# Turning the first two blocks of rows before the second permutation, in a one-core transformer kernel

## The chip, the cores and the metric

The kernel runs on one core of a Trainium2 chip. The metric is device microseconds for one execution, and the median of several executions is compared.

## The reference

The input x is 2 sequences of 1024 rows by 256 columns. Four steps follow one another; each adds its result, times the tanh of a gate, to x. What matters here is the second step, a mixture of experts with 2 of 16 experts for each row:

```python
x = x + tanh(g_xattn[0]) * attention(layernorm(x), ctx, ctx)
# second step, on h = layernorm(x), 2048 rows
scores = softmax(h @ gate_w); topk_w, topk_idx = top_k(scores, 2)
y = sum over the 2 picked e of topk_w * ((silu(h @ w1[e]) * (h @ w3[e])) @ w2[e])
x = x + tanh(g_ffn[0]) * (y + h)
x = x + tanh(g_xattn[1]) * linear_of(layernorm(x), mean of ctx)
x = x + tanh(g_ffn[1]) * ternary_mlp(layernorm(x))     # 256 -> 1024 -> 1024 -> 1024 -> 256
```

## The kernel before, in words

**Stages.** The attention and the routing take the first 66 us of the profile, the expert blocks come next, and four groups of 512 rows go through the last network. That last network is one long run of matmuls on TensorE.

**Blocks.** The 4096 picks (2048 rows, two experts each) are sorted by expert into up to 47 blocks of 128 rows (`NBLK`). The first 16 blocks are the first 128 picks of each expert, so that block i belongs to expert i; the other 31 (`NREST`) hold what is left. The list of a block's rows (`perm`) is made by a product of 0/1 matrices on TensorE, which the code calls a permutation: `ohr` says at which place in its block a pick stands, `ohf` and `ohb` say in which block. The first permutation (with `ohf`) fills the lists of the 16 blocks, the second (with `ohb`) those of the other 31. GpSimd reads the lists and fetches the rows of each block from HBM with an indirect DMA into one of six buffers (`xg`, `xg_more`).

**One block.** TensorE turns the 128 x 256 rows (`turns`, two transposes), ScalarE copies the high part out (`high_turned`), VectorE takes the remaining low part (`low`), and TensorE multiplies both with the expert's weights (`gate_up`, six matmuls). ScalarE's SiLU and VectorE's `product` follow, and the product rides along with the turning of a later block to the expert's second product (`down`). Loops on all engines run over i, the block, and `turns` is called two blocks ahead: `turns(0)` and `turns(1)` stand ahead of the loop.

**The order.** Every engine's work is written out by hand in one list. An engine takes its list in order, and semaphores make it wait for other engines. What the change touches stands at one place in the program, between the first permutation and the loop over the blocks:

- VectorE makes `ohb` in some 25 steps, then ten small steps compute the expert of each of the 31 blocks (`ecol`), then come `low(0)` and `low(1)`.
- TensorE fills waits with products that nobody reads, `keep_clock(bank, n)`: n calls of 128 x 128 by 128, each of which stands as two rows in the profile. It does the first permutation in two pieces with such fillers between them, fillers again, the second permutation, one small product for the experts' offsets (`pe_eoff`), two fillers, and the two turns.
- The turned halves lie in `turned0` to `turned5`, and `turned0` to `turned4` lie over `ohr`. The second permutation reads `ohr`, so with these buffers a turn can be copied out only after it.
- A turn waits for the rows that GpSimd fetched, and all turns stand behind a wait for `pool_step` 3, which GpSimd gives after it has issued the first fetch.

Of the kernel before, what the change touches and what calls it, by code (L numbers as in the profile page):

```python
# [29 lines left out]
P = 128  # L30
# [81 lines left out]
def flamingo_kernel(nc, x, ctxT, cols, rows, wq, wkT, wvT, gate, experts, w1T, w2T, panels, consts, identity, out):  # L112
    with ExitStack() as ctx:
# [89 lines left out]
        route_end = w_off + 4 * 4 * DK * D  # L203
        VT = put("VT", [P, DK, P])
# [9 lines left out]
        xT = put("xT", [P, 2, DK, GN])  # L214
# [64 lines left out]
        t_high, t_low = turned[0:3], turned[3:6]  # L279
        outb = nc.alloc_sbuf_tensor_at("outb", [P, TG, D], F32, offset=bl_off)  # L280
# [61 lines left out]
        bank_y, bank_first = [bank[6], bank[5]], bank[7]  # L342

# [404 lines left out]
        def _(eng):  # L748
# [276 lines left out]
            own(eng.tensor_scalar(bexp[:, :], pinc_0[:, :], 1.0 / P, kc[:, K_TOK:K_TOK + 1], ALU.mult, ALU.is_le))  # L1025
            own(eng.tensor_tensor(ends_0[:, :], count_0[:, 0:E], prest_0[0:1, :], ALU.add))
            own.done()
            own(eng.reduce_sum(ecol_0[:, :], bexp[:, :], AX.X))

            own(eng.scalar_tensor_tensor(count_0[:, 0:E], count_0[:, 0:E], float(P), ends_0[:, :], ALU.is_gt, ALU.mult))  # L1030
            own.done()
            own(eng.tensor_scalar(bexp[:, :], pinc[:, :], 1.0 / P, kc[:, K_TOK:K_TOK + 1], ALU.mult, ALU.is_le))
            own(eng.scalar_tensor_tensor(ecol_0[:, :], ecol_0[:, :], float(E), ecol_0[:, :], ALU.is_lt, ALU.mult))
            own.done()
            own(eng.reduce_sum(ecol[:, :], bexp[:, :], AX.X))
            own.done()
            own(eng.tensor_tensor(ecol[:, :], ecol[:, :], ecol_0[:, :], ALU.add))
            own.done()
            eng.tensor_scalar(ecol[:, :], ecol[:, :], float(E - 1), float(EXP_COLS), ALU.min, ALU.mult).then_inc(dve_ecol, 1)
            own(eng.reduce_max(end_0[:, :], count_0[:, :], AX.X))  # L1040

# [61 lines left out]
            def low(n):  # L1103
                b, w = n % 3, joint(n)
                eng.wait_ge(b_xh, n + 1)
                eng.tensor_tensor(t_low[b][:, w], bank_t[b][:, w], t_high[b][:, w].bitcast(F32),  # L1106
                                  ALU.subtract).then_inc(b_xl, 1)
# [60 lines left out]
            low(0)  # L1168
            low(1)
# [180 lines left out]
        def _(eng):  # L1350
# [126 lines left out]
            def high_turned(n):  # L1477
                b, w = n % 3, joint(n)
                eng.wait_ge(b_tx, n + 1)
                eng.activation(t_high[b][:, w], bank_t[b][:, w], ACT.Copy).then_inc(b_xh, 1)  # L1480
# [102 lines left out]
        def _(eng):  # L1583
# [205 lines left out]
            def first_there(r, t):  # L1789
# [49 lines left out]
            def gate_up(i, at_):  # L1839
                b = i % 3  # L1840
# [4 lines left out]
                for k in range(DK):  # L1845
                    w = bass.ds(at_ + k * 2 * H, 2 * H)
                    x_k = slice(k * P, (k + 1) * P)
                    ins = three(bank_gu[i % 2][:, 0:2 * H], (t_high[b][:, x_k], t_low[b][:, x_k]), (EH[:, w], EL[:, w]),
# [42 lines left out]

            eng.wait_ge(act_setup, ACT_LATE + 2)

            eng.wait_ge(pool_step, 3)
            keep_clock(bank[5], 2)
            turns(0)
            turns(1)
            for i in range(NBLK + DOWN):
                expert_there(i)
                if i < 2:  # L1900
                    gate_up(i, offsets[i])
                    turns(i + 2)
                else:
# [240 lines left out]
```

## Time and profile before

| what | us |
|---|---|
| median of 3 executions | 500.75 |
| the three executions | 500.48, 500.75, 505.57 |
| the profiled execution's own time | 505.3 |
| its span, first to last instruction | 503.2 |
| time of the profiled execution outside the span | 2.1 |

The granted clock of TensorE has two levels in the profile, 1.00 (2.4 GHz) and 0.50 (1.2 GHz); its mean over the span is 0.975. A stretch at the lower level makes TensorE's work there take about twice as long. The profiled execution is one of the longer ones: it lies 4.55 us above the median, and near the longest of the three.

### The profile page before, as it was taken

Reading aid. Unit: us, or ns where it says so; the run is one execution under the profiler, and the core shown is the slowest. Engines: PE = TensorE matmul, PEld = TensorE weight load, DVE = VectorE, ACT = ScalarE, POOL = GpSimd, SP = SyncE. Lnnn points to the kernel's source line nnn. Section 1 sums busy time; section 2 is a strip of 40 time slices with the busy share of each in tenths; the row PEclk is TensorE's granted clock in tenths of the full one; section 3 lists DMA queues with packets and bytes.
Section 4 is the critical chain, followed back from the end, with each engine's and each line's share of the span. In section 5 each row is a group of like instructions: output and inputs, shape, how many; then the busy total and the mean of one; then the engine's idle time right before and its main releaser. Section 6 shows DMA issues by size and latency. Waiting matters only on the chain.

```text
span 503.2 us, 7823 instructions
## 1 busy us (share of the span) xinstructions
PE 482.0 (96%) x2742; PEld 415.2 (83%) x2742; DVE 317.0 (63%) x848; ACT 217.9 (43%) x444; POOL 150.7 (30%) x157
## 2 busy tenths in 40 slices
PE   8898979998798999999999999999999999999996
PEld 8787769997787788888978888887888898788885
DVE  4868886875686766656476776346875634654523
ACT  4568935775467876411362221236112223511210
POOL 1667867747870411100260111044110101000000
PEclk9879977999999999999999999999999999999999
DMA  8944833797663578212050320022132002022101
GB/s 294 350 173 139 283 122 105 221 305 230 203 190 115 178 261 271 64 42 85 3 167 21 106 63 2 0 70 98 24 102 64 1 1 83 4 81 66 40 1 49
DMA packets 34465, 58.82 MB, mean 117 GB/s; under 512 B 4529, under 2 KB 18353, under 8 KB 34354
## 3 DMA queue, kind: packets, MB, share of 16 engines
q1 hardware_dynamic: 29760, 47.12, 28.9%
q0 software_dynamic: 3840, 10.49, 7.3%
q10 hardware_dynamic: 818, 0.61, 0.5%
q8 instruction: 25, 0.41, 0.4%
q14 instruction: 22, 0.18, 0.1%
HBM read 47.85 MB, written 14.42 MB: 124 GB/s over the span
## 4 chain that ended last, share of the span: by engine, by line
PE 84%; DVE 8%; POOL 3%; DMA 2%; issue 2%; ACT 0%; SPq 0%; DVEq 0%
PE bank L2015 23%; PE bank L2016 23%; PE bank L1984 6%; PE bank L1987 6%; PE bank L1588 3%; PE bank L1590 3%; PE bank L1589 3%; PE bank L2048 3%; PE bank L2047 3%; PE bank L1833 2%; DMA xg<-xb_dram,perm 2%; PE bank L1648 1%; PE bank L1681 1%; DMA gw<-gate 1%; POOL y_first L623 1%
## 5 line engine op out<-in xcount | busy, mean ns | idle before, releaser
L1562 ACT ACTIVATE sg<-bank,colv 128x512 f32<-128x512 f32 x64 | 44.1, 690 | 176.6 <-PE bank L2016 176.6
L2015 PE MATMUL bank<-Ah,Wr 128*128 128x512 f32 x256 | 100.2, 391 | 0.0
L2015 PE MATMUL bank<-Bh,Wr 128*128 128x512 f32 x256 | 99.9, 390 | 0.0
L2016 PE MATMUL bank<-Al,Wr 128*128 128x512 f32 x256 | 99.7, 390 | 0.0
L2016 PE MATMUL bank<-Bl,Wr 128*128 128x512 f32 x256 | 99.7, 389 | 0.0
L2015 PEld LDWEIGHTS bank<-Ah,Wr 128*128 128x128 f32 x256 | 48.0, 188 | 11.1 <-DVE Al L1275 0.8
L2016 PEld LDWEIGHTS bank<-Bl,Wr 128*128 128x128 f32 x256 | 48.1, 188 | 9.9
L2015 PEld LDWEIGHTS bank<-Bh,Wr 128*128 128x128 f32 x256 | 48.1, 188 | 9.8
L2016 PEld LDWEIGHTS bank<-Al,Wr 128*128 128x128 f32 x256 | 48.1, 188 | 9.7
L1288 DVE CAST Ah<-sg 128x512 fp32r<-128x512 f32 x32 | 13.6, 425 | 60.1 <-ACT sg L1562 60.1
L1588 PE MATMUL bank<-EL,turned 128*128 (+1 forms) x141 | 44.9, 319 | 0.9 <-DVE turned L1106 0.6
L565 POOL TENSOR_TENSOR rstd<-veps,mhalf 128x4 f32<-128x4 f32 x6 | 8.4, 1399 | 107.9 <-DVE veps L745 61.1
L1590 PE MATMUL bank<-EH,turned 128*128 (+1 forms) x141 | 40.5, 287 | 0.0
L1589 PE MATMUL bank<-EH,turned 128*128 (+1 forms) x141 | 40.5, 287 | 0.0
L1548 ACT ACTIVATE sg<-bank,colv 128x512 f32<-128x512 f32 x32 | 22.1, 690 | 38.1 <-PE bank L1987 37.6
L1271 DVE SCALAR_TENSOR_TENSOR sg<-bank,colv,sg 128x512 f32<-128x512 f32 x32 | 24.0, 751 | 22.9 <-ACT sg L1548 22.6
L1288 DVE CAST Bh<-sg 128x512 fp32r<-128x512 f32 x32 | 13.6, 426 | 38.6 <-ACT sg L1562 38.6
L1984 PE MATMUL bank<-xTh,Wr 128*128 128x512 f32 x96 | 37.7, 393 | 0.0
L1987 PE MATMUL bank<-xTl,Wr 128*128 128x512 f32 x96 | 37.6, 392 | 0.0
L642 POOL DMA_INDIRECT xg<-xb_dram,perm x32 | 31.3, 979 | 10.1 <-issue 6.0
L1480 ACT ACTIVATE turned<-bank 128x384 fp32r<-128x384 f32 (+2 forms) x51 | 23.8, 467 | 20.4 <-PE bank L1836 11.6
L1106 DVE TENSOR_TENSOR turned<-bank,turned 128x384 fp32r<-128x384 f32 (+2 forms) x51 | 26.6, 521 | 9.3 <-ACT turned L1480 9.0
(286 smaller groups left out, 1039.8 us busy)
## 6 DMA issues: line engine op xcount, KB each, us to landing
Wraw<-panels SPq DMA_DIRECT2D x44, 256.0 KB, 4.0
stage<-panels SPq DMA_DIRECT2D x44, 256.0 KB, 2.7
ES<-experts SPq DMA_DIRECT2D x16, 384.0 KB, 5.4
ys_dram<-yb SPq DMA_DIRECT2D x47, 128.0 KB, 2.7
ys_dram<-x SPq DMA_DIRECT2D x1, 1920.0 KB, 8.7
X<-x SPq DMA_DIRECT2D x3, 512.0 KB, 7.1
xb_dram<-xb SPq DMA_DIRECT2D x3, 512.0 KB, 5.3
out<-outb SPq DMA_DIRECT2D x3, 512.0 KB, 3.3
```

The costliest lines, as they stand in the source:

```text
L642: eng.indirect_dma_start(out=rows, out_offset=None, in_=xb_dram, in_offset=bass.IndirectOffsetOnAxis(ap=perm[:, i:i + 1], axis=0)).then_in ...
L1106: eng.tensor_tensor(t_low[b][:, w], bank_t[b][:, w], t_high[b][:, w].bitcast(F32), ALU.subtract).then_inc(b_xl, 1)
L1271: eng.scalar_tensor_tensor(sg[:, m % 3, :], bank[2 * (m % 2) + 1][:, :], colv[:, C_S2 + m:C_S2 + m + 1], sg[:, m % 3, :], ALU.mult, ALU.mu ...
L1288: own(eng.tensor_copy(h[0][:, m, :], sg[:, r, :]))
L1562: eng.activation(sg[:, (8 * layer + m) % 3, :], bank[m % 4][:, :], ACT.Gelu, scale=colv[:, c + m:c + m + 1]).then_inc(f_act[m], 1)
L1588: mm(dst, lhs[0], rhs[1], start=first, stop=False)
L1589: mm(dst, lhs[1], rhs[0], start=False, stop=False)
L1590: return mm(dst, lhs[0], rhs[0], start=False, stop=last)
L1984: mm(dst, w[:, u, k, :], x_high[:, k, :], start=k == 0, stop=False)
L1987: ins = mm(dst, w[:, u, k, :], x_low[:, k, :], start=False, stop=k == DK - 1 and not general)
L2015: mm(bank[m % 4][:, :], Wr[:, base:base + P], h[0][:, k, :], start=k == 0, stop=False)
L2016: ins = mm(bank[m % 4][:, :], Wr[:, base:base + P], h[1][:, k, :], start=False, stop=k == FK - 1 and not general)
```

## The change

Two pairs of buffers, `first_high` and `first_low`, take the turned halves of blocks 0 and 1. They lie where `xT` of the attention lay, which is moved to the front of its region for that, so `ohr` is no longer in the way. On TensorE `turns(0)` and `turns(1)` stand ahead of the second permutation. The fillers are 8 in place of 4 between the pieces of the first permutation, and 9 and 10 in place of 12 ahead of the second; the 2 after it are gone. The small product for the offsets goes behind `turns(3)`. On VectorE the ten `ecol` steps stand behind `low(0)`, ahead of `low(1)`.

```diff
+        put = over(route_end, e_off)
+        first_high, first_low = ([put(f"{n}{b}", [P, DK * P], F32R) for b in range(2)] for n in ("first_high", "first_low"))
...
+        def turned_pair(n):
+
+            return (first_high[n], first_low[n]) if n < 2 else (t_high[n % 3], t_low[n % 3])
...
@@ VectorE
-            own(eng.tensor_scalar(bexp[:, :], pinc_0[:, :], 1.0 / P, kc[:, K_TOK:K_TOK + 1], ALU.mult, ALU.is_le))
...
-            own(eng.reduce_max(end_0[:, :], count_0[:, :], AX.X))
...
             low(0)
+            own(eng.tensor_scalar(bexp[:, :], pinc_0[:, :], 1.0 / P, kc[:, K_TOK:K_TOK + 1], ALU.mult, ALU.is_le))
...
+            own(eng.reduce_max(end_0[:, :], count_0[:, :], AX.X))
             low(1)
...
@@ TensorE
                     if t == NT - TG:
-                        keep_clock(bank[5], 4)
+                        keep_clock(bank[5], 8)
                         eng.wait_ge(dve_ohf, NG)
...
-            keep_clock(bank[5], 12)
...
-            permutation(bank_y[0][:, 0:NREST], lambda r, t: ohb[:, r, :, t], rest_there)
-
-            eng.wait_ge(dve_ecol, 1)
-            mm(bank_first[0:1, 0:NREST], ecol[:, :], ident[:, 0:NREST], start=True, stop=True).then_inc(pe_eoff, 1)
...
+            keep_clock(bank[5], 9)
             eng.wait_ge(act_setup, ACT_LATE + 2)
-
             eng.wait_ge(pool_step, 3)
-            keep_clock(bank[5], 2)
+            keep_clock(bank[1], 10)
             turns(0)
             turns(1)
+            permutation(bank_y[0][:, 0:NREST], lambda r, t: ohb[:, r, :, t], rest_there)
             for i in range(NBLK + DOWN):
...
                     turns(i + 2)
+                    if i == 1:
+                        eng.wait_ge(dve_ecol, 1)
+                        mm(bank_first[0:1, 0:NREST], ecol[:, :], ident[:, 0:NREST], start=True, stop=True).then_inc(pe_eoff, 1)
```

This is TensorE's list before, from the first permutation (`ohf`) to the first block's gate/up products. `xg_more` and `xg` with `ident` are the turns, `ohb` is the second permutation, and a call of `keep_clock` is one `bank<-ident`:

```order
L1786 MATMUL bank<-ohf,ohr 128x16 x24
L1595 MATMUL bank<-ident 128x128 x4
L1786 MATMUL bank<-ohf,ohr 128x16 x8
L1595 MATMUL bank<-ident 128x128 x12
L1786 MATMUL bank<-ohb,ohr 128x31 x32
L1814 MATMUL bank<-ident,ecol 1x31
L1595 MATMUL bank<-ident 128x128 x2
L1833 MATMUL bank<-ident,xg_more 128x128 x2
L1833 MATMUL bank<-ident,xg 128x128 x2
L1588 MATMUL bank<-EL,turned_183 128x256
```

And the same place after the change, where the lines of the code stand about six further on:

```order
L1792 MATMUL bank<-ohf,ohr 128x16 x24
L1601 MATMUL bank<-ident 128x128 x8
L1792 MATMUL bank<-ohf,ohr 128x16 x8
L1601 MATMUL bank<-ident 128x128 x19
L1831 MATMUL bank<-ident,xg_more 128x128 x2
L1831 MATMUL bank<-ident,xg 128x128 x2
L1792 MATMUL bank<-ohb,ohr 128x31 x32
L1594 MATMUL bank<-EL,first_high_189 128x256
```

The two turns moved ahead of the permutation, with all the fillers ahead of them, and the gate/up product of block 0 stands right behind the permutation.

This is VectorE's list after the change, from the end of `ohb` to the first `product`; before it, rows `bexp` to `end_173` stood directly behind `ohb`:

```order
L1027 TENSOR_TENSOR ohb<-kbrep,pblk_143 128x496 x2
L1096 TENSOR_TENSOR first_low_191<-bank,first_high_189 128x256
L1158 TENSOR_SCALAR bexp<-pinc_163,kc 128x16
...
L1172 TENSOR_SCALAR ecol<-ecol 128x1
L1173 TENSOR_REDUCE end_173<-count_172 1x1
L1096 TENSOR_TENSOR first_low_192<-bank,first_high_190 128x256
L1100 TENSOR_TENSOR bh<-bank,bsg 128x128
```

The low part of block 0 now stands ahead of the expert steps, that of block 1 behind them.

## Rows read from the trace of the kernel before

**Rows 1.** The page, part 4: engines' shares of the chain that ended last.

```profile
PE 84%; DVE 8%; POOL 3%; DMA 2%; issue 2%; ACT 0%; SPq 0%; DVEq 0%
```

**Rows 2.** Windows: length, then PE, PEld, DVE, ACT, POOL busy; PEclk, DMA, GB/s.

```profile
21.20:31.40 10.20, 10.20 (x43) 9.43 (x42) 7.12 (x34) 5.06 (x14) 8.12 (x11) 0.50 0.85 306
31.40:65.50 34.10, 30.94 (x259) 25.67 (x259) 28.37 (x122) 30.93 (x71) 25.67 (x34) 1.00 0.57 185
65.50:72.40 6.90, 5.80 (x32) 5.41 (x32) 6.30 (x32) 1.70 (x3) 2.86 (x4) 0.51 0.28 88
72.40:75.80 3.40, 2.66 (x38) 2.52 (x39) 2.41 (x13) 0.00 (x0) 2.53 (x3) 1.00 0.40 119
75.80:82.60 6.80, 6.20 (x30) 5.83 (x29) 2.87 (x10) 2.58 (x7) 4.71 (x5) 0.50 0.32 97
82.60:110.00 27.40, 27.40 (x236) 27.34 (x236) 23.38 (x70) 20.70 (x57) 19.52 (x19) 1.00 0.74 228
```

**Rows 3.** The chain that ended last, 73 to 84 us: start, us, what.

```profile
73.14 2.06 PE bank L1786 x32
75.19 0.15 PE bank L1814 x2
75.34 0.70 PE bank L1595 x4
76.04 0.44 PE bank L1833 x2
...
76.51 0.39 ACT turned L1480
...
76.92 0.43 DVE turned L1106
...
77.49 0.55 PE bank L1588
...
82.52 0.21 PE bank L1588
82.74 0.12 PE bank L1589
```

**Rows 4.** Timeline of TensorE: start, us, work, [idle before it, ended by].

```profile
41.45 0.20 PE L1689 MATMUL bank<-both,tri 128*128 128x64 f16 x1 [1.25 <-DVE both L842]
...
62.76 1.14 PE L1595 MATMUL bank<-ident 128*128 128x128 f32 x8
65.45 0.25 PE L1786 MATMUL bank<-ohf,ohr 128*128 128x16 f16 x4 [1.55 <-DVE ohr L894]
66.25 0.28 PE L1786 MATMUL bank<-ohf,ohr 128*128 128x16 f16 x4 [0.56 <-DVE ohr L894]
66.38 5.47 PE L1595 MATMUL bank<-ident 128*128 128x128 f32 x24
73.14 2.06 PE L1786 MATMUL bank<-ohb,ohr 128*128 128x31 f16 x32 [1.29 <-DVE ohb L1021]
...
83.86 0.38 PE L1833 MATMUL bank<-ident,xg_more 128*128 128x128 f32 x2
```

**Rows 5.** Timeline of VectorE at the same place.

```profile
72.58 0.74 DVE L1021 TENSOR_TENSOR ohb<-kbrep,pblk 128x496 f16<-128x496 f16 x2
73.24 0.23 DVE L1025 TENSOR_SCALAR bexp<-pinc,kc 128x16 f32<-128x16 f32 x1
...
74.89 0.15 DVE L1040 TENSOR_REDUCE end<-count 1x1 f32<-1x17 f32 x1
```

**Rows 6.** Timeline of GpSimd: issues of the fetches, and a later wait.

```profile
69.14 1.29 POOL L642 DMA_INDIRECT xg_more<-xb_dram,perm  x1 [3.43 <-DMA xb_dram<-xb]
70.73 1.06 POOL L642 DMA_INDIRECT xg<-xb_dram,perm  x1 [0.30 <-issue]
...
77.09 0.94 POOL L642 DMA_INDIRECT xg_more<-xb_dram,perm  x1 [0.30 <-PE bank L1833]
...
112.74 1.16 POOL L623 DMA_INDIRECT y_first<-ys_dram,slots  x1 [4.69 <-DMA ys_dram<-yb]
```

**Rows 7.** The tile xg between 60 and 84 us: its DMA from issue to landing.

```profile
DMA to landing us min/median/max: 2.8/2.8/2.8
```

More of the change, by code:

```diff
@@ L203, in flamingo_kernel @@
         route_end = w_off + 4 * 4 * DK * D
+        xT = put("xT", [P, 2, DK, GN])
         VT = put("VT", [P, DK, P])
@@ L213, in flamingo_kernel @@
         ones128 = put("ones128", [P, P])
-        xT = put("xT", [P, 2, DK, GN])
         xb = put("xb", [P, 2, TG, D])
@@ L1022, in _ @@
                                   pblk16[:, r, :].unsqueeze(1).to_broadcast([P, NREST, NT]), ALU.is_equal).then_inc(dve_ohb, 1)
-            own(eng.tensor_scalar(bexp[:, :], pinc_0[:, :], 1.0 / P, kc[:, K_TOK:K_TOK + 1], ALU.mult, ALU.is_le))
[L1026 to L1039, printed above, removed]
-            own(eng.reduce_max(end_0[:, :], count_0[:, :], AX.X))
             def block_experts():
@@ L1104, in low @@
                 b, w = n % 3, joint(n)
+                high_, low_ = turned_pair(n)
                 eng.wait_ge(b_xh, n + 1)
-                eng.tensor_tensor(t_low[b][:, w], bank_t[b][:, w], t_high[b][:, w].bitcast(F32),
-                                  ALU.subtract).then_inc(b_xl, 1)
+                eng.tensor_tensor(low_[:, w], bank_t[b][:, w], high_[:, w].bitcast(F32), ALU.subtract).then_inc(b_xl, 1)
             def product(i):
@@ L1168, in _ @@
             low(0)
+            own(eng.tensor_scalar(bexp[:, :], pinc_0[:, :], 1.0 / P, kc[:, K_TOK:K_TOK + 1], ALU.mult, ALU.is_le))
+            own(eng.tensor_tensor(ends_0[:, :], count_0[:, 0:E], prest_0[0:1, :], ALU.add))
+            own.done()
+            own(eng.reduce_sum(ecol_0[:, :], bexp[:, :], AX.X))
+            own(eng.scalar_tensor_tensor(count_0[:, 0:E], count_0[:, 0:E], float(P), ends_0[:, :], ALU.is_gt, ALU.mult))
+            own.done()
+            own(eng.tensor_scalar(bexp[:, :], pinc[:, :], 1.0 / P, kc[:, K_TOK:K_TOK + 1], ALU.mult, ALU.is_le))
+            own(eng.scalar_tensor_tensor(ecol_0[:, :], ecol_0[:, :], float(E), ecol_0[:, :], ALU.is_lt, ALU.mult))
+            own.done()
+            own(eng.reduce_sum(ecol[:, :], bexp[:, :], AX.X))
+            own.done()
+            own(eng.tensor_tensor(ecol[:, :], ecol[:, :], ecol_0[:, :], ALU.add))
+            own.done()
+            eng.tensor_scalar(ecol[:, :], ecol[:, :], float(E - 1), float(EXP_COLS), ALU.min, ALU.mult).then_inc(dve_ecol, 1)
+            own(eng.reduce_max(end_0[:, :], count_0[:, :], AX.X))
             low(1)
@@ L1479, in high_turned @@
                 eng.wait_ge(b_tx, n + 1)
-                eng.activation(t_high[b][:, w], bank_t[b][:, w], ACT.Copy).then_inc(b_xh, 1)
+                eng.activation(turned_pair(n)[0][:, w], bank_t[b][:, w], ACT.Copy).then_inc(b_xh, 1)
             def silu(i):
@@ L1839, in gate_up @@
             def gate_up(i, at_):
-                b = i % 3
+                high_, low_ = turned_pair(i)
                 eng.wait_ge(b_xl, i + 1)
@@ L1847, in gate_up @@
                     x_k = slice(k * P, (k + 1) * P)
-                    ins = three(bank_gu[i % 2][:, 0:2 * H], (t_high[b][:, x_k], t_low[b][:, x_k]), (EH[:, w], EL[:, w]),
+                    ins = three(bank_gu[i % 2][:, 0:2 * H], (high_[:, x_k], low_[:, x_k]), (EH[:, w], EL[:, w]),
                                 k == 0, k == DK - 1)
```

## The prediction

> **What bounds the kernel now.** I read the chain of waits first, from the end back. TensorE holds 84% of it [rows 1], so whatever lets TensorE reach its dense work sooner, or gives it a faster clock, should move the end, and work of other engines counts only where TensorE stands still for it. Next come the windows, for the granted clock. TensorE is at half clock in two places near the change, 65.5 to 72.4 us and 75.8 to 82.6 us, with full clock in the 3.4 us between [rows 2]. In the first nothing but fillers and waits is at stake. In the second it does the first blocks' real products, 6.20 us of work in 6.80 us, and each six-matmul product costs double: a matmul follows the last after 0.21 us at half clock and after 0.12 us at full [rows 3].
>
> Then the chain itself, piece by piece between 73 and 78 us [rows 3]. The second permutation runs from 73.14 to 75.19, the small product for the offsets takes 0.15, the two fillers 0.70, two of the four transposes 0.44, and then the chain leaves TensorE: ScalarE copies the high part of block 0 (76.51), VectorE takes the low part (76.92), and gate/up of block 0 starts at 77.49. So 2.30 us pass between the permutation's end and the first product (77.49 - 75.19), for work that needs nothing from the permutation. Ahead of it TensorE has stood 1.29 us for `ohb` [rows 4], after 5.47 us of fillers. The transposes would fit there if the rows of blocks 0 and 1 have come.
>
> **When the turns can run after the change.** Three things hold them up: the fillers ahead of them, the rows, and `pool_step`.
>
> The rows: GpSimd issues the fetch of block 0 at 69.14 and that of block 1 at 70.73 [rows 6]; a fetch lands 2.8 us after its issue [rows 7]. Block 0 is there at about 71.9 and block 1 at 73.53. Nothing ahead of these two fetches changes. GpSimd's signal comes behind the first issue, at 69.14 + 1.29 = 70.43.
>
> The fillers: 24 rows, 12 calls, took 5.47 us at half clock [rows 4], or 0.456 us for a call, and so about 0.228 at full. The nine calls from 66.38 end at 70.48 at half clock and at 68.43 at full; the ten calls behind the signal then start at about 70.45 in either case. At full clock they end at 72.7. At half clock until 72.4, as now, 4.2 calls fit before that and the other 5.8 take 1.3 us: 73.7. At half clock all the way they end at 75.0.
>
> With full clock the turns of block 0 end at 72.95 and TensorE waits for block 1 until 73.53; its turns end at 73.75 (0.22, half of the 0.44 of [rows 3]). `ohb` is ready at 73.00 for its first half and at 73.3 for its second [rows 3, 5], so the permutation starts at 73.75 and ends at 75.80 (its 2.05 us of now). That is 0.6 us later than now. With the clock as now up to 72.4, the turns end at 74.2 and the permutation at 76.25.
>
> Which of the two? Between 62.8 and 66.4 TensorE now stands 1.55 and 0.56 us, with four fillers' 1.14 us ahead [rows 4], and the clock falls by 65.5 to 65.6 [rows 2]. Four more calls fill 0.91 of the 1.55. The nearest row on the other side is the wait of 1.25 us at 41.45, through which the clock held [rows 4, 2]; 0.64 us idle is less than that, so I take the full clock. The doubt is worth 76.25 - 75.80 = 0.45 us, and a new idle time of about 2 us opens between the nine and the ten fillers (68.43 to 70.43), longer than the 1.25 that I know to be harmless.
>
> **Engines beside it.** ScalarE is idle from its table load on, so the high part of block 0 is done by 73.4. `low(0)` waits for it at the head of VectorE's list, behind `ohb` which ends at 73.3, and is done at 73.85 (its 0.43). What is queued behind it on VectorE is the ten steps of `ecol`, now 73.24 to 75.04 [rows 5], where VectorE then idles until 76.92. They now run from about 73.85 to 75.65, and `low(1)` ends at 76.1. Who waits for that? Gate/up of block 1, at 75.80 + 0.72 + 0.22 = 76.7 or later (six matmuls at 0.12, the turns of block 2), so the 1.8 us are still hidden; the cover goes if the first turns come after 74.5. The product for the offsets stands behind `turns(3)`, needs `ecol` of 75.6, and keeps its 0.15 us. The fetches of blocks 2 to 5 are issued as now. The other buffers' places and the copy of the low part into `first_low` cost nothing: same shapes, same engines.
>
> **First term, the order.** Gate/up of block 0 finds its low part ready since 73.85 and starts with the end of the permutation at 75.80 in place of 77.49: 1.69 us. Checked by pieces: 2.30 us between permutation and product go, less the 0.6 us by which the permutation starts later. With the slower fillers it is 77.49 - 76.25 = 1.24.
>
> **Second term, the clock in the blocks.** Now the clock falls at 75.8, at the end of a stretch with 2.66 us busy of 3.40 [rows 2], most of it the permutation's narrow matmuls (31 columns), and comes back at 82.6, some 5.1 us after the first product. The changed kernel has the same permutation there, and nearly the same wait, so I expect the fall again. But then TensorE has dense products at once, where it now begins with fillers, transposes and the wait for turned halves until 77.49. The shortest stretch at one level in the rows is 3.4 us [rows 2]; I estimate that the half clock lasts 3.4 us from 75.8 in place of 6.8. Products now spend 5.1 us at half clock, then 3.4, and half of the difference is gained: 0.86 us. The bounds are a half clock of the same 6.8 us, which loses (6.8 - 5.1)/2 = 0.85 of the first term, and no fall at all, which gains 5.1/2 = 2.55. I take the value in between because the wait inside the stretch is gone but the permutation before it is not.
>
> **Sum.** 1.69 + 0.86 = 2.55 us. In the trace that brings the turns of block 6 from 83.86 [rows 4] to 81.3. They need the fetch issued at 77.09 [rows 6], there at 79.9, so the supply holds and caps the whole gain at about 4. From 82.6 on TensorE has no idle time up to 110 [rows 2]; the following wait of GpSimd for the stored results (4.69 us at 112.74 [rows 6]) is for blocks that TensorE finishes, and so moves with it. I expect all of the 2.55 us at the end.
>
> **One rule weighed.** The second fetch sets the start of the permutation: 70.73 + 2.8 = 73.53 [rows 6, 7]. The Trainium skill, DMA: Bandwidth & Descriptors, section Anatomy of one DMA, gives a GpSimd DMA about 2.0 us plus its bytes at 436 GB/s, an estimate of 2.3 us for these 128 KB. By it the rows would be there at 73.0 and the first term would be 2.2 us; the trace has 2.8, and I keep that.
>
> **Against which time.** The profiled execution took 505.3 us, 4.55 above the median, so by its own time the changed kernel would show 502.75. The clock was at half for 10.20 us from 21.2 on [rows 2], before anything that the change touches, and half of that, 5.1 us, is about what lies between the two short executions (500.48, 500.75) and the longest. I take it that the short ones did not fall there. The change has no part in it, but it may set on which side a median falls. From the median: 500.75 - 2.55 = 498.2.
>
> **The rivals.** *The clock never falls.* If the fillers and turns keep the clock up through the permutation, the gain is 1.69 + 2.55 = 4.2, capped at 4 by the supply: 496.7. For it speaks that more of the stretch ahead is filled; against it, that the permutation's 2.05 us of narrow work and a wait remain.
>
> *The order helps, the clock takes it back.* The fall comes as now and lasts as long: 1.69 - 0.85, or 1.24 - 0.85 with slow fillers, 0.4 to 0.8: 500.1. Or the early turns gain nothing because block 1's rows land later than the eight other fetches say; then 500.5.
>
> *Slower: fillers ahead of the work.* The ten calls stand directly ahead of `turns(0)`. If the clock is low all the way from 65.5, they end at 75.0, the turns at 75.9, the permutation at 78.0 and gate/up starts at 78.1, 0.6 us late; if the clock then comes back one 3.4 us stretch later than now, at 86.0, products spend 7.9 us at half clock in place of 5.1, or 1.4 us more. Together 2.0 us: 502.8. It decides once the fillers end after 74.9. For it speaks the idle time of 2 us; against it, that 5.47 us of fillers brought the clock back at 72.4, and that the new list has more of them.
>
> *The median on the long side.* Two of four executions seen are at 505.3 to 505.6. With 2.55 gained the median would be 502.8 if most of the measured ones fall at 21 us.
>
> **How the numbers follow.** Forecast, gain 1.5 to 3.5: 0.45. No fall: 0.15. Little or nothing, 0 to 1.5: 0.15. Slower fillers: 0.08. Long side: 0.17. Predicted time 498.2. The range leaves out the lower end of the no-fall case and the worst of the last two: 496.0 to 503.2. A measurement of this kernel can tell about 1% (5 us) from no change, as the three times before spread by that much. Faster by over 1% needs 495.7: the no-fall case with luck in the executions, 0.09. Slower by over 1% needs 505.8: slow fillers and the long side together, 0.05. Within 1%: 0.86.
>
> **What the profile after would show.** The turns of blocks 0 and 1 end near 73.75, with a wait for the fetch of block 1 ahead of the second. The permutation follows without a wait for `ohb`, and gate/up of block 0 directly behind it with no wait for `first_low`. VectorE's `low(0)` is ahead of `bexp`, and nobody waits for `low(1)`. The half clock before the blocks is gone or shorter, and the one behind the permutation ends near 79. The turns of block 6 come near 81.3. I am wrong if ten fillers end after 74, if gate/up of block 1 waits for VectorE, or if a clock fall as long as 6.8 us follows gate/up of block 0.

## The result and the profile after

The changed kernel takes 497.78 us, the median of 22 executions (496.02 to 503.03); the kernel before takes 500.54 us beside it (22 executions, 499.08 to 505.72). The ratio is 0.9946, with a 95% interval of 0.9923 to 0.9968: a gain of 2.76 us, and between 1.6 and 3.9 by the interval. The forecast was 498.2.

The profiled execution took 501.49 us with a span of 499.6, 3.6 less than the span before. First the windows, with the columns of [rows 2]. The lines of the code stand some six further on than before.

```profile
8.00:14.80 6.80, 6.47 (x31) 6.48 (x32) 5.04 (x18) 2.54 (x6) 3.12 (x5) 0.50 1.05 378
...
65.50:72.40 6.90, 5.27 (x44) 4.69 (x44) 6.28 (x31) 1.70 (x3) 2.64 (x3) 1.00 0.22 65
72.40:75.80 3.40, 2.63 (x39) 2.62 (x39) 2.44 (x14) 0.77 (x2) 2.48 (x4) 1.00 0.33 101
75.80:82.60 6.80, 6.80 (x61) 6.57 (x60) 5.68 (x16) 4.62 (x13) 5.28 (x6) 1.00 0.39 115
82.60:110.00 27.40, 26.64 (x227) 26.25 (x226) 22.60 (x70) 20.72 (x56) 19.14 (x20) 1.00 0.85 261
```

Both half-clock stretches beside the change are gone: 61 matmuls between 75.8 and 82.6 us where [rows 2] have 30. There is one new thing in the last row: 0.76 us of idle time in 27.4, where TensorE had none. The timeline of TensorE after (start, us, work, idle before and what ended it) answers to [rows 4]:

```profile
65.76 0.26 PE L1792 MATMUL bank<-ohf,ohr 128*128 128x16 f16 x4 [0.56 <-DVE ohr L900]
65.87 2.25 PE L1601 MATMUL bank<-ident 128*128 128x128 f32 x18
69.08 2.47 PE L1601 MATMUL bank<-ident 128*128 128x128 f32 x20 [0.95 <-POOLq L652]
71.97 0.44 PE L1831 MATMUL bank<-ident,xg_more 128*128 128x128 f32 x2 [0.42 <-DMA xg_more<-xb_dram,perm]
73.17 0.44 PE L1831 MATMUL bank<-ident,xg 128*128 128x128 f32 x2 [0.77 <-DMA xg<-xb_dram,perm]
73.45 2.06 PE L1792 MATMUL bank<-ohb,ohr 128*128 128x31 f16 x32
75.32 0.37 PE L1594 MATMUL bank<-EL,first_high 128*128 128x256 f32 x1
...
79.66 0.38 PE L1831 MATMUL bank<-ident,xg_more 128*128 128x128 f32 x2
...
90.14 0.41 PE L1831 MATMUL bank<-ident,xg 128*128 128x128 f32 x2 [0.49 <-DMA xg<-xb_dram,perm]
...
97.61 0.41 PE L1831 MATMUL bank<-ident,xg_more 128*128 128x128 f32 x2 [0.27 <-DVE turned L1096]
...
115.03 0.41 PE L1831 MATMUL bank<-ident,xg_more 128*128 128x128 f32 x2 [1.81 <-DMA xg_more<-xb_dram,perm]
```

The order is as written: fillers, the two turns, the permutation, and the product of block 0 with no wait at all. The chain of waits (start, us, what) now reaches the permutation through the fetch of block 1, and no longer through VectorE and ScalarE as in [rows 3]:

```profile
63.90 4.48 DMA xb_dram<-xb
...
69.15 0.96 POOL xg_more L648
70.11 0.30 issue
70.41 2.72 DMA xg<-xb_dram,perm
73.17 0.44 PE bank L1831 x2
73.61 1.89 PE bank L1792 x32
75.51 0.18 PE bank L1594
```

VectorE's timeline, against [rows 5]: the low part of block 0 follows `ohb` at once, the last of the ten steps is over at 74.75, and the low part of block 1 comes behind it; no row of TensorE waits for either.

```profile
72.05 0.74 DVE L1027 TENSOR_TENSOR ohb<-kbrep,pblk 128x496 f16<-128x496 f16 x2
72.86 0.42 DVE L1096 TENSOR_TENSOR first_low<-bank,first_high 128x256 fp32r<-128x256 f32 x1
...
74.60 0.15 DVE L1173 TENSOR_REDUCE end<-count 1x1 f32<-1x17 f32 x1
74.68 0.40 DVE L1096 TENSOR_TENSOR first_low<-bank,first_high 128x256 fp32r<-128x256 f32 x1
```

GpSimd's fetches and its later wait, against [rows 6]:

```profile
69.15 0.96 POOL L648 DMA_INDIRECT xg_more<-xb_dram,perm  x1 [3.93 <-DMA xb_dram<-xb]
70.41 0.94 POOL L648 DMA_INDIRECT xg<-xb_dram,perm  x1 [0.30 <-issue]
...
108.97 0.99 POOL L629 DMA_INDIRECT y_first<-ys_dram,slots  x1 [2.74 <-DMA ys_dram<-yb]
```

**One mark to measure from.** Executions reach the change at different times, so absolute times of two traces can't be subtracted. All places below are therefore counted from the start of the last four matmuls of the first permutation (66.25 us before, 65.76 after), which both lists have and behind which the change acts. "First product" is gate/up of block 0, "turns 6" the turns of block 6, "y of 15" the end of ScalarE's copy of block 15's result, "fetch of y" GpSimd's first fetch of stored results, and "last network" its first fetch of `xn`. The span is the mark, plus the place of the last network, plus what follows.

| kernel | span | mark | first product | turns 6 | y of 15 | fetch of y | last network | what follows |
|---|---|---|---|---|---|---|---|---|
| before | 503.2 | 66.25 | 11.24 | 17.61 | 40.68 | 46.49 | 99.91 | 337.04 |
| after | 499.6 | 65.76 | 9.56 | 13.90 | 38.07 | 43.21 | 96.89 | 336.95 |

The 3.6 us of the two spans are 0.49 ahead of the change, 3.02 in the blocks, and 0.09 behind. The last network takes the same time in both, as in all executions below that ran on like chips (336.8 to 337.2), so whatever a version gains it must have by then.

### The profile page after: what moved, and what is told of

The parts are those of the page before. It is cut to its first block, busy times and chain, and to the rows that moved or that the text cites. A ratio compares the mean times of both kernels' runs of the same rounds, so it can differ in the third digit from the quotient of the medians.

```text
span 499.6 us, 7859 instructions
## 1 busy us (share of the span) xinstructions
PE 474.8 (95%) x2760; PEld 409.5 (82%) x2760; DVE 316.6 (63%) x848; ACT 217.9 (44%) x444; POOL 149.0 (30%) x157
## 4 chain that ended last, share of the span: by engine, by line
PE 79%; DVE 7%; DMA 5%; POOL 5%; issue 2%; ACT 0%; ACTq 0%; DVEq 0%; POOLq 0%
PE bank L2017 23%; PE bank L2018 23%; PE bank L1986 6%; PE bank L1989 6%; PE bank L2050 3%; PE bank L2049 3%; PE bank L1594 2%; PE bank L1596 2%; PE bank L1595 2%; DMA xg<-xb_dram,perm 2%; POOL y_first L629 2%; POOL xg_more L648 1%; POOL xg L648 1%; DMA colv<-cols 1%; PE bank L1831 1%
## 5 line engine op out<-in xcount | busy, mean ns | idle before, releaser
L1594 PE MATMUL bank<-EL,turned 128*128 (+1 forms) x137 | 42.6, 311 | 0.3 <-ACT yb L1500 0.3
L1596 PE MATMUL bank<-EH,turned 128*128 (+1 forms) x137 | 38.7, 283 | 0.0
L1554 ACT ACTIVATE sg<-bank,colv 128x512 f32<-128x512 f32 x32 | 22.1, 690 | 38.1 <-PE bank L1989 37.6
L1595 PE MATMUL bank<-EH,turned 128*128 (+1 forms) x137 | 38.6, 282 | 0.0
L1269 DVE SCALAR_TENSOR_TENSOR stage<-stage,Wr 128x512 f32<-128x512 f32 x44 | 30.1, 685 | 1.9 <-DMA stage<-panels 1.8
```

Source lines behind the costliest of these rows:

```text
L1269: eng.scalar_tensor_tensor(stage[:, w % 2, :], stage[:, w % 2, :], 1.0, to.bitcast(F32), ALU.mult, ALU.not_equal, accum_out=diff[:, w:w + ...
L1594: mm(dst, lhs[0], rhs[1], start=first, stop=False)
L1595: mm(dst, lhs[1], rhs[0], start=False, stop=False)
L1596: return mm(dst, lhs[0], rhs[0], start=False, stop=last)
```

## The experiments

All of them start from the changed kernel unless another is named. Each one's program has a constant (the 64 that it comes to with these inputs) where GpSimd waits for a number of stored blocks that it loads, ahead of the fetch of y. Most ratios rest on 12 executions of the kernel and 18 to 35 of the kernel before on the same chip. The experiments ran on four chips: one for the constant alone, the fillers alone, the old fillers and block 1's turns inside; a second for one filler, 25, the steps first and the turns behind; a third for the two versions with later panels and the one with results one block later; and a fourth for all three edits at once. The constant alone ran on the first only, so a version on another chip is set against it by the two ratios and by the places in the traces.

**The changed kernel with that constant alone.**

```diff
-                        eng.wait_ge(dma_ys[b], stored_n[b])
+                        eng.wait_ge(dma_ys[b], 16 * (E // 4))
```

> The changed kernel with one edit that all my kernels have: GpSimd's wait for the stored results of the first 16 blocks is written as the constant 64 for each of four semaphores, in place of the counts that it loads (for these inputs they are 64). Every theory: no difference from the changed kernel. Ratio to the kernel before 0.995, from the start of the first permutation to the turns of block 6 about 18.0 us (21.7 before), no half clock between 62 and 110 us.

Measured: 499.69 us against 500.58, ratio 0.9983 (0.9951 to 1.0016), where 0.995 was expected, and with a half clock where none was expected. The first product comes at 9.50, as in the changed kernel, but turns 6 at 15.30 in place of 13.90. The windows say why:

```profile
61.70:71.00 9.30, 7.21 (x75) 6.61 (x76) 8.40 (x42) 2.47 (x5) 5.21 (x5) 1.00 0.30 87
71.00:74.40 3.40, 3.40 (x22) 3.40 (x20) 0.94 (x4) 0.66 (x2) 2.50 (x3) 0.51 0.38 101
```

The clock fell at 71.0, just ahead of the first product at 71.20, and for 3.4 us. The edit acts some 30 us later, so this is the same list on TensorE with the other outcome: no fall (13.90) or one of 3.4 us (15.30). The executions differ in the same sense: the mean granted clock of one execution has the median 0.994 in the changed kernel, 0.988 with the constant alone, and 0.986 in the kernel before beside it. Whether chance, the chip or the constant makes the 0.006 between the first two was not tried. Five more of the versions below on like chips show that short fall at this place. This kernel, and not the changed one, is what the others are read against; the two ratios' intervals overlap, and that is how much one ratio says.

**The fillers alone, and the order without them.** In the kernel before, 8 fillers in place of 4 between the pieces of the first permutation:

```diff
-                        keep_clock(bank[5], 4)
+                        keep_clock(bank[5], 8)
```

> The kernel before with 8 fillers in place of 4 between the pieces of the first permutation, nothing else. Theory 1 (the gain is the order, and a clock that holds because of the order and the fillers together): the 12 calls now run at full clock and end near 69, TensorE then stands 4 us for ohb, the clock is low when the first products run, and nothing is gained: ratio 1.000 (0.998 to 1.003), stretch to the turns of block 6 21 to 23 us. Theory 2 (the gain is the clock, and the fillers alone give it): ratio 0.996 or less, stretch 19 to 20 us.

The changed kernel with the numbers of before (4, 12, and the 2 ahead of `turns(0)`):

```diff
-                        keep_clock(bank[5], 8)
+                        keep_clock(bank[5], 4)
...
-            keep_clock(bank[5], 9)
+            keep_clock(bank[5], 12)
...
-            keep_clock(bank[1], 10)
+            keep_clock(bank[1], 2)
```

> The changed kernel's order with the fillers of before: 4 between the pieces of the first permutation, 12 ahead of the wait for GpSimd's signal, 2 behind it. Theory 1: the order's 1.7 us stay, the clock falls near 65.5 and is low for one stretch among the first products or fewer: stretch 18 to 20 us, ratio 0.995 to 0.9975. Theory 2 (fillers are what gains): the order alone gives nothing, ratio 1.000, stretch over 21 us.

Measured: the fillers alone 501.47 us, ratio 1.0007 (0.9977 to 1.0036); first product at 11.73, turns 6 at 17.22. The order with the old fillers 499.26 us (one of its 12 executions took 943 us), ratio 0.9975 (0.9943 to 1.0006); first product at 9.51, turns 6 at 15.30, the same two places as with the new fillers. In the trace of the fillers alone

```profile
63.52 2.92 PE L1595 MATMUL bank<-ident 128*128 128x128 f32 x24
70.28 2.06 PE L1786 MATMUL bank<-ohb,ohr 128*128 128x31 f16 x32 [3.83 <-DVE ohb L1021]
...
75.14 0.55 PE L1588 MATMUL bank<-EL,turned 128*128 128x256 f32 x1 [0.60 <-DVE turned L1106]
```

the 24 filler rows run at full clock, in 2.92 us where [rows 4] have 5.47, and all that they leave is a longer wait for `ohb`, 3.83 us in place of 1.29. The new order makes the first term; the new counts of fillers make none of it.

**One filler, and 25.** In place of 8, 9 and 10, a single call; and 25 in place of the last 10:

```diff
-                        keep_clock(bank[5], 8)
...
-            keep_clock(bank[5], 9)
...
-            keep_clock(bank[1], 10)
+            keep_clock(bank[1], 1)
```

> The changed order with no fillers between the pieces of the first permutation and one call in place of 9 and 10 ahead of the turns. P is the start of the last four matmuls of the first permutation; from P to the turns of block 6 it took 17.6 us in the kernel before, 13.9 in the changed kernel, 15.3 in its repeat with a clock fall. Theory (fillers hold the clock, the order gives its part alone): first product still 9.5 to 9.9 us behind P since the rows of block 1 set it, at half clock for 3.4 to 7 us: 15.5 to 17 us to the turns of block 6, ratio 0.997 to 1.000. Rival (fillers are worth nothing): 14 to 15.3 us, ratio 0.9945.

```diff
-            keep_clock(bank[1], 10)
+            keep_clock(bank[1], 25)
```

> The changed kernel with 25 calls in place of 10 directly ahead of the turns of block 0. It tests the rival of the prediction that ends slower, fillers ahead of the work, and whether a delay at this place reaches the end. At full clock 15 calls more are 3.4 us, 2.1 of which lie in what were waits for rows: first product about 11.5 us behind P in place of 9.7, the turns of block 6 at 15.7 (17.2 with a clock fall). If everything passes to the end: 1.8 us over the changed kernel, ratio to before 0.998 to 1.000. If the stages behind absorb it: ratio 0.9945 to 0.996.

Measured: one filler 498.26 us, ratio 0.9955 (0.9926 to 0.9984), nearer to the rival's 0.9945 than to the theory's 0.997 to 1.000. The clock is at half from 60.2 to 73.9 us, through all waits, both turns and the permutation, and yet the first product comes at 9.71 and turns 6 at 15.13, which is the rival's place too. With 25: 497.67 us, ratio 0.9950 (0.9929 to 0.9972). In its trace

```profile
67.91 5.82 PE L1601 MATMUL bank<-ident 128*128 128x128 f32 x50 [0.84 <-POOLq L652]
...
74.00 2.06 PE L1792 MATMUL bank<-ohb,ohr 128*128 128x31 f16 x32
```

the fillers end at 73.73, so the permutation starts at 9.3 behind the mark in place of 7.6, and the first product at 11.17. The clock then holds, and turns 6 come at 15.50: from product to turns 6 it is 4.33 us, as in the changed kernel's trace (4.34), against 5.80 with the short fall. So of the 1.6 us that the surplus fillers cost, 1.5 come back with the full clock, and the bill is even. It is not the luck of one trace: over the 12 executions of each, the mean granted clock has the median 0.984 with one filler and 0.998 with 25, and the ratios are 0.9955 and 0.9950.

**Block 1's turns inside the permutation.** They no longer hold the permutation's first half:

```diff
                 if t == 0:
+                    if r == 1:
+                        turns(1)
                     eng.wait_ge(dve_ohb, r + 1)
...
             turns(0)
-            turns(1)
```

> The changed kernel with the turns of block 1 moved from ahead of the second permutation into it, behind its first 12 matmuls. The permutation then starts behind the turns of block 0 and not behind the landing of block 1's rows, where TensorE waited 0.77 us. Theory 1 (the first products start earlier, but the fetch of block 6, issued at 76.7 and landing 2.7 us later, caps what follows): the first product starts 0.7 to 0.9 us earlier, the turns of block 6 only 0.3 us, ratio to before 0.994. Rival (nothing else is short): all of 0.8 us stays, stretch 17.2 us, ratio 0.993.

Measured: 497.47 us, ratio 0.9943 (0.9916 to 0.9970). TensorE's timeline:

```profile
67.69 0.44 PE L1833 MATMUL bank<-ident,xg_more 128*128 128x128 f32 x2 [0.64 <-DMA xg_more<-xb_dram,perm]
68.47 0.87 PE L1792 MATMUL bank<-ohb,ohr 128*128 128x31 f16 x12 [0.34 <-DVE ohb L1027]
69.16 0.41 PE L1833 MATMUL bank<-ident,xg 128*128 128x128 f32 x2
...
80.39 0.41 PE L1833 MATMUL bank<-ident,xg 128*128 128x128 f32 x2 [0.41 <-DMA xg<-xb_dram,perm]
```

The wait for block 1's rows is gone, the first product comes at 8.89 (0.6 earlier), the clock never falls, and turns 6 come at 13.74. But the turns at 80.39 us, those of block 9, wait for their rows, and y of 15 comes at 38.04, only 0.34 ahead of the constant-only version's 38.38. Behind that start the fetches are the next limit.

**VectorE's ten steps ahead again, and the turns behind again.** First `low(0)` moved back behind the ten steps:

```diff
-            low(0)
             own(eng.tensor_scalar(bexp[:, :], pinc_0[:, :], 1.0 / P, kc[:, K_TOK:K_TOK + 1], ALU.mult, ALU.is_le))
...
+            low(0)
             low(1)
```

> The changed kernel with VectorE's ten expert steps ahead of the low part of block 0, as before the change. They take 1.5 to 1.8 us and end at 8.5 to 8.9 us behind P, the low part by 9.2; the permutation ends at 9.6 to 9.7. Theory: nobody waits, first product and turns of block 6 as in the changed kernel (13.9, or 15.3 with a fall), ratio 0.9945. Rival (the order on VectorE carries part of the gain): first product 0.4 to 1.2 us later, with a wait for first_low ahead of it.

In a version of its own, with VectorE's list as changed, both turns behind the permutation, into the new buffers all the same:

```diff
+            permutation(bank_y[0][:, 0:NREST], lambda r, t: ohb[:, r, :, t], rest_there)
             turns(0)
             turns(1)
-            permutation(bank_y[0][:, 0:NREST], lambda r, t: ohb[:, r, :, t], rest_there)
```

> The changed kernel with both turns behind the second permutation again; fillers, the place of the offsets' product, buffers and VectorE's list stay as changed. It prices the position of the turns alone. Theory: the permutation starts when ohb is ready, 6.8 us behind P, ends at 8.8, then turns 0.44, ScalarE 0.4, VectorE 0.43 and the hand-overs: first product 10.2 to 10.4 us behind P in place of 9.7, so only 0.6 us of the 1.7 is the position and the rest the two fillers and the offsets' product that stood behind the permutation: turns of block 6 at 14.5 (16 with a fall), ratio 0.996. Rival (the position is the whole gain): first product 11.2 us behind P, ratio 0.999 or more.

Measured: the steps first 498.99 us, ratio 0.9972 (0.9946 to 0.9999), first product 9.39, turns 6 15.19: nothing lost, the ten steps fit ahead of the first product either way. The turns behind 499.98 us, ratio 0.9981 (0.9954 to 1.0009):

```profile
71.79 0.35 PE L1594 MATMUL bank<-EL,first_high 128*128 128x256 f32 x1 [0.81 <-DVE first_low L1096]
...
73.69 0.36 PE L1594 MATMUL bank<-EL,first_high 128*128 128x256 f32 x1 [0.74 <-DVE first_low L1096]
```

The permutation now starts at 6.80, 0.8 earlier, and the product waits 0.81 us for the low part as before; it comes at 10.12. So of the 1.7 us of the first product, the place of the turns is worth 0.6; the other 1.1 are the rest of the edit, which this version keeps. 0.85 of them are the two fillers and the offsets' product that stood between permutation and products (0.70 and 0.15 in [rows 3]); it isn't the place of `low(0)`, since the steps-first version loses nothing. The 0.74 further down is block 1, whose low part stands behind the ten steps. The clock held here, and that pays for both waits: turns 6 come at 15.41.

**The loads of panels later.** While the blocks run, SyncE's queue holds loads of the last network's weights (`panels`) between the stores of the blocks' results, and GpSimd's 4.69 us of [rows 6] wait for the last of these stores. The loads are spread to later blocks, and VectorE's conversion of four of the panels is moved behind them, to blocks 26 to 29:

```diff
-PAN_DVE = tuple(range(16, 24))
+PAN_DVE = (16, 17, 18, 19, 26, 27, 28, 29)
...
-            panel_at = [PAN_AT + 3 * (w // 2) + w % 2 if w < DVE_PAN else PAN_AT + 12 + 2 * (w - DVE_PAN) for w in range(NRAW)]
+            panel_at = [8, 9, 11, 12, 19, 21, 23, 25, 27, 28, 29, 30, 32, 34, 36, 38]
```

> The changed kernel with the loads of weight panels 4 to 15 from SP's queue moved later (panels 4 to 7 from blocks 14, 15, 17, 18 to 19, 21, 23, 25, the others behind them) and VectorE's rounding of panels 4 to 7 behind that. It asks where the rest of the gain of the first blocks went. GpSimd starts to fetch the stored results 43.2 to 44.6 us behind P (the start of the last four matmuls of the first permutation) in all variants of the changed order, whether the turns of block 6 came at 13.7 or at 15.5; it waits 2.7 to 4.5 us there for the store of the first 16 blocks, which share the DMA engines and SP's queue with the panels. Theory (panel traffic delays these stores, and that wait takes the early blocks' gain back): the fetch starts at 41.5 to 42.5, the last network 1.5 to 2 us earlier behind P than 96.7 to 98.0, ratio to before 0.990 to 0.993. Rival (the stores are set by TensorE's pace): fetch at 43.2 or more, ratio 0.995 to 0.998.

The same loads together with block 1's turns inside the permutation:

> The later panels of the run before this one together with the turns of block 1 inside the second permutation. With the wait for the stores gone, the 0.2 to 0.7 us by which the first blocks are earlier should reach the end: ratio 0.0005 to 0.0015 below that of the later panels alone, 0.989 to 0.992. Rival (GpSimd's fetches set the pace anyway): the same ratio as with the later panels alone.

Measured: alone 496.38 us (8 executions, 494.88 to 498.3), ratio 0.9902 (0.9866 to 0.9937), the lowest ratio of all. Its interval lies below that of the constant-only version, and its upper end just reaches into that of the changed kernel. Together with block 1's turns inside the permutation 497.88 us, ratio 0.9935 (0.9899 to 0.9971). SyncE's queue in the changed kernel, and then with the later loads, where the seven stores stand in a row with no load between them:

```profile
101.05 0.32 SPq L468 DMA_DIRECT2D ys_dram<-yb  x1
101.41 1.32 SPq L369 DMA_DIRECT2D Wraw<-panels  x1
102.78 1.40 SPq L468 DMA_DIRECT2D ys_dram<-yb  x2
104.22 0.47 SPq L369 DMA_DIRECT2D Wraw<-panels  x1
```

```profile
94.30 8.74 SPq L468 DMA_DIRECT2D ys_dram<-yb  x7
103.08 0.43 SPq L369 DMA_DIRECT2D Wraw<-panels  x1
```

From the end of ScalarE's copy of block 15 to GpSimd's fetch it is 3.73 us (99.89 to 103.62) with the later loads alone, and 3.72 in the combination, against 5.14 in the changed kernel and 5.81 before. The fetch of y comes at 42.04 and 41.51, the last network at 95.64 and 95.32. In the combination the first product (8.90) and the last network are the earliest of all, but its ratio of 0.9935 lies above both expectations; the intervals overlap, so these executions do not rank the two.

The places show the path, and the ratio shows less. Against the constant alone the last network comes 2.4 us earlier (98.04 to 95.64), and the two ratios are 0.0081 apart, which is 4 us, on different chips. The kernel with the old loads and results as before did not run on this third chip. And all 8 executions with the later loads alone had a mean clock of 0.992 or more, where 5 of the 12 of each of the other two versions on this chip had 0.983 to 0.989. So a part of the 0.9902 may be the clock's luck and not the loads.

**The results added one block later.**

```diff
-Y_AT = (28, 29, 31, 32, 34, 35, 37, 38)
+Y_AT = (29, 30, 31, 32, 34, 35, 37, 38)
```

> The changed kernel with GpSimd's first fetch of stored results, and its wait for the stores, one block later (29, 30, 31, 32 in place of 28, 29, 31, 32), so that the rows of block 29 are fetched in the wait. If that wait holds GpSimd up and GpSimd sets the pace from there to the last network: GpSimd saves up to 1.2 us of its list, and TensorE's wait of 1.8 us for the rows of block 29 goes: ratio 0.992 to 0.995. If VectorE's addition of these results at block 25 is what TensorE waits for then: no gain or a loss, ratio 0.995 to 0.999.

Measured: 497.46 us, ratio 0.9910 (0.9876 to 0.9944), with the last network at 97.02. A fetch of rows more stands ahead of GpSimd's wait, so TensorE's wait for the fetch queued behind it shrinks to 0.38 us at 111.83 (1.81 in the changed kernel, 2.63 in the constant-only version). In its place TensorE stands for VectorE, which now takes up the results while TensorE wants its product:

```profile
114.59 0.33 PE L1834 MATMUL bank<-ident,bh 128*128 128x128 f32 x1 [2.35 <-DVE bh L1100]
```

The first theory had the wait for the rows right, and its rival the wait for VectorE. The ratio came out below what either expected, and the trace does not explain it: its last network, at 97.02, is no earlier than in other versions with the old loads (96.7 to 98.0). What makes that ratio, one of three near 0.99 on the same chip, stays open.

**All three edits at once.**

> The changed kernel with three edits at once: the turns of block 1 inside the first product, the loads of the last network's panels spread to later blocks, and the y of each block one block later. Theory (what the fetch of the stored results sets at the end of the blocks passes through whole, and the three edits act at different places): behind the start of the last four matmuls of the first permutation the first product comes at 8.9 us, the turns of block 6 at 13.7 to 14.7 us, GpSimd's first fetch of stored results at 42 to 43 us, and the last network begins at 94.3 to 95.3 us; ratio to the kernel before 0.986 to 0.989. Rival (the later y sets GpSimd's fetch behind one fetch of x more, and VectorE's additions then come beside the last blocks' other work and hold TensorE): the fetch of stored results no earlier than 43.5 us, the last network from 96.5 us, and the ratio 0.990 or above, so that the later loads of the panels alone stay the best.

By "inside the first product" it means inside the second permutation; the edit is the one above.

Measured: 513.16 us against 513.69 for the kernel before on the same chip, ratio 0.9987 (0.9956 to 1.0018). On this chip the kernel before takes 12 to 13 us more than in the other comparisons. The trace of this version shows where such time goes: in the window from 72 to 152 us TensorE is busy for 69.30 of 80 us (72.76 with the constant alone), and some of its waits have no releaser in the profile, only "issue".

```profile
72.00:152.00 80.00, 69.30 (x492) 63.57 (x492) 51.06 (x145) 38.40 (x119) 52.90 (x55) 0.92 0.63 187
```

```profile
76.21 0.38 PE L1833 MATMUL bank<-ident,xg 128*128 128x128 f32 x2 [0.99 <-issue]
77.64 0.38 PE L1833 MATMUL bank<-ident,xg 128*128 128x128 f32 x2 [0.90 <-issue]
```

The first product comes at 9.98, turns 6 at 20.39, y of 15 at 46.69 and the last network at 110.96. One thing carries over: from y of 15 to the fetch of y it is 3.77 us, as with the later loads elsewhere. By its numbers the version falls to the rival (a fetch of y after 43.5, the last network after 96.5, a ratio above 0.990). But the trace doesn't test either reason: with the blocks 8 us later, the waits that the edits remove are not those that hold this chip. Whether the three add up stays open, and so does what is slow on that chip.

The marks of the versions on like chips, for the argument that follows:

| version | mark | first product | turns 6 | y of 15 | fetch of y | last network | ratio |
|---|---|---|---|---|---|---|---|
| constant alone | 61.70 | 9.50 | 15.30 | 38.38 | 44.10 | 98.04 | 0.9983 |
| fillers alone | 63.41 | 11.73 | 17.22 | 40.29 | 45.29 | 100.89 | 1.0007 |
| old fillers | 61.67 | 9.51 | 15.30 | 38.37 | 43.77 | 97.35 | 0.9975 |
| turns 1 inside | 61.67 | 8.89 | 13.74 | 38.04 | 43.17 | 97.20 | 0.9943 |
| one filler | 61.73 | 9.71 | 15.13 | 38.21 | 43.23 | 96.91 | 0.9955 |
| 25 fillers | 64.70 | 11.17 | 15.50 | 38.57 | 44.13 | 97.73 | 0.9950 |
| steps first | 61.54 | 9.39 | 15.19 | 38.27 | 43.19 | 96.71 | 0.9972 |
| turns behind | 61.67 | 10.12 | 15.41 | 38.49 | 44.61 | 97.97 | 0.9981 |
| panels later | 61.58 | 9.52 | 15.23 | 38.31 | 42.04 | 95.64 | 0.9902 |
| inside and panels | 67.42 | 8.90 | 14.71 | 37.79 | 41.51 | 95.32 | 0.9935 |
| y one later | 62.18 | 9.41 | 15.21 | 38.29 | 43.74 | 97.02 | 0.9910 |

## Why the prediction was right, and where it was not

**The first term, the order (1.69 us), was right.** The first product comes 1.68 us earlier behind the mark (11.24 to 9.56), and the path to it is the forecast one: the turns of block 1 wait for their fetch (70.41 + 2.72), then the permutation, then the product without a wait. The estimate that a moved permutation costs 0.6 was near too: with the turns behind it, it starts 0.8 earlier. For the fetch the measured 2.8 us of [rows 7] was the value to keep: the trace after has 2.72. The estimate from the Trainium skill (DMA: Bandwidth & Descriptors, Anatomy of one DMA) was 2.3, and this trace does not agree with it.

**GpSimd's signal was put too late.** I had it behind the first issue, 4.2 us behind the mark. It released TensorE's ten fillers at 69.08, 3.3 behind it, at the time at which the issue starts. The idle time that I feared between the fillers was 0.95 us and not 2. It cost nothing either way, since the fetch of block 1 bounds the turns.

**The second term, the clock in the blocks, was mis-sized, since it has two values and not one.** I took 0.86 us, a fall of 3.4 us at the first product. The profiled execution of the changed kernel has no fall, and the term there is 2.03 us (3.71 at turns 6 less 1.68); with the constant alone the fall is there as forecast, and the term is 0.57 (2.31 less 1.74). The forecast's 81.3 us for turns 6 is 15.05 behind the mark; eight versions came at 15.1 to 15.5 (with a short fall, a half clock until some 12 us behind the mark, a late product or a wait), the combination with panels (a short fall, but an early product) at 14.71, and only the trace after and the one with block 1's turns inside, without any of these, at 13.7 to 13.9. The rival of a clock that never falls thus happened in the trace after, and the forecast in most of the others.

**"I expect all of the 2.55 us at the end" was right in size and wrong in its reason.** Three things stand between turns 6 and the end. First, waits take away what exceeds some 2.6 us: turns 6 are 3.71 us early in the trace after and y of 15 only 2.61; with the short fall 2.31 and 2.30. The blocks follow each other every 1.40 us, and the trace after loses that pace twice: 0.64 us at 90.14, where TensorE reaches the fetches (0.49 us for `xg`), and 0.43 at 97.61, where it waits for VectorE's low part. The row at 80.39 of block 1's turns inside shows the fetches again. The cap was forecast at 4 us, from the issue at 77.09 of block 6 alone, with no wait for VectorE in it. It is not a fixed one either: the combination with panels has y of 15 2.89 us early (40.68 to 37.79) and none of these waits. So the lucky clock is worth 0.3 us at y of 15, and not 1.4. Then GpSimd's wait does not simply move with TensorE: it ends 5.81 us behind y of 15 before, and 4.9 to 6.1 us in the versions with the old loads, as the store meets the loads of panels. That spread is wider than the difference between no fall and a short one. It is also where 1.4 us were to be had: 3.7 with the later loads. From the fetch of y to the last network it is 53.3 to 54.0 us in all but the version with the fillers alone (55.6), and from there on 336.8 to 337.2.

So it is partly luck that 2.76 us were measured where 2.55 were forecast. In the trace after, a clock term larger than forecast and losses that were not forecast nearly cancel; with the constant alone, the clock term is smaller and the ratio gives 0.9 us. The seven versions with the new order and the old loads and results that ran on the first two chips have ratios from 0.9943 to 0.9983, which are gains of 0.9 to 2.9 us.

**"Fillers ahead of the work" did not happen, and fillers did not help.** The 25 show the price that I gave that rival: a first product 1.6 us late. They also show its return, a full clock afterwards. Whether 1, 18, 27 or 42 calls stand there, y of 15 comes at 38.1 to 38.6.

**The cause of long and short executions was half found.** The forecast put 4.55 us of the profiled execution to a half clock at 21.2 to 31.4 us. Where the mark comes early (61.5 to 62.2, eight of the versions on like chips) there is none ahead of 60 us. The clocks of all executions agree: of the 35 of the kernel before beside the first four versions, the four above 504 us have a mean clock of 0.969 to 0.975, and the others 0.979 to 0.992. But there is a wait as well. In the trace of the constant alone and in that of the fillers alone, which has no fall either and a mark 1.7 us later:

```profile
19.50 0.63 PE L1664 MATMUL bank<-ident,pr 128*64 128x128 f32 x4 [0.16 <-DVE pr L827]
```

```profile
21.20 0.63 PE L1658 MATMUL bank<-ident,pr 128*64 128x128 f32 x4 [1.40 <-DVE pr L821]
```

TensorE waits 1.40 us for VectorE there in the kernel before too, and with 25 fillers and in the combination with panels; in the last three the clock falls behind it (marks 66.25, 64.70, 67.42). The trace after is long for a third reason: its first product waits 2.73 us for a first load, until 8.32 us, and the clock falls there until 14.86 (first window above). It ends 3.71 us above the median, as the one before it did by 4.76. What decides between these in an execution was not tried.

## What to carry to other kernels

Place every step against a mark that both lists share, and follow a gain from stage to stage: here 3.7 us at block 6 were 2.6 at block 15, because TensorE had reached the fetches and VectorE. When an engine waits for a stored result, look at what stands between the stores on that queue: in these traces moving loads that nobody waits for yet brought the last network 1.2 to 2.4 us forward, on top of 1.9 to 3.0 by the reordering, and the version with both ran at 0.990 of the time before (0.987 to 0.994). Fillers that keep a clock up are worth a run with one of them and a run with many before they are tuned by the call.

## What the runs showed of the hardware that was not expected

The granted clock is not a function of the list alone: the kernel before had mean clocks from 0.969 to 0.992 in 35 executions on one chip, and the same order on TensorE ran into the first products at full clock in one trace and at half clock for 3.4 us in another. With one filler it was at half from 60.2 to 73.9 us, and so came back about when it did behind the short falls of other versions on nearly the same mark (74.1 to 74.7): the first products had a half clock for about as long, and 26 calls fewer cost nothing. The stored 128 KB of a block could be fetched from 3.7 us after its data were ready with no other load near it on the queue, and after 4.9 to 6.1 with them. And one chip ran the kernel before in 513.7 us where the others took 500.5 to 501.3, and the version traced there shows waits of about 1 us that no recorded event ends.
